# A four-layer graph network: node tables written inside the edge passes, normalizations in halves

## The reference, cut to what matters

```
h = relu(layernorm(x));  x = x + GAT(h)        # two graph attention passes over the edges:
    xl, xr = h @ Wl.T + bl, h @ Wr.T + br
    score  = leaky(xl[src] + xr[dst] + edge_attr @ We.T) @ att
    alpha  = softmax of score over the edges of a target
    out    = segment_sum(alpha * xl[src], dst) + bo
    g = instance_norm(relu(out1));  g = instance_norm(relu(out2(g) + h @ Wskip.T + bskip))
h = relu(layernorm(x));  x = x + GIN(h)        # neighbour sums, MLP, batch norm over the nodes, relu, + h
h = relu(layernorm(x));  x = x + ATT(h)        # attention over the edges, then a layer norm
h = relu(layernorm(x));  x = x + GCN(GCN(h))   # two normalized neighbour sums with an MLP between
```

## Time and profile before

| | us |
|---|---|
| time before, median of 3 runs (lowest to highest) | 6561.05 (6558.09 to 6562.64) |
| profiled execution, its own time | 6555.38 |
| its span from first to last instruction | 6553.5 |
| PE / DVE / ACT / POOL busy | 5634.2 / 4266.8 / 2346.2 / 3061.3 |
| granted TensorE clock, mean share of full speed | 0.947 |

### The profile page before, as it was taken

The page is one execution under the profiler, slowest core; times in us unless marked ns, Lnnn a source line. Parts: engine busy times, 40 slices in busy tenths (PEclk is TensorE's granted clock), DMA queues, the critical chain, the costliest instruction groups (busy, mean ns, idle before and its releaser), DMA issues. The chain is left out here.

```text
span 6553.5 us, 176947 instructions
## 1 busy us (share of the span) xinstructions
PE 5634.2 (86%) x42237; PEld 3858.0 (59%) x42238; DVE 4266.8 (65%) x13369; ACT 2346.2 (36%) x4950; POOL 3061.3 (47%) x3216
## 2 busy tenths in 40 slices
PE   0399999999999938999999999996785999994978
PEld 0366666666666626666666666664773333334978
DVE  5477777777777766777777777776326666665131
ACT  0144444444444414444444444442002444441000
POOL 0177777777777707777777777772000000000000
PEclk9999999999999959999999999997876999996979
DMA  1244444444444414444444444441741222222948
GB/s 47 55 113 106 107 107 109 107 108 107 107 107 108 110 29 109 107 109 107 107 108 108 108 107 107 109 106 36 309 172 40 90 95 90 84 81 104 379 183 308
DMA packets 706049, 768.34 MB, mean 117 GB/s; under 512 B 375941, under 2 KB 628909, under 8 KB 680885
## 3 DMA queue, kind: packets, MB, share of 16 engines
q1 hardware_dynamic: 584087, 583.69, 29.5%
q0 software_dynamic: 102400, 105.06, 8.5%
q10 hardware_dynamic: 19488, 78.68, 3.1%
HBM read 678.14 MB, written 88.81 MB: 117 GB/s over the span
## 5 line engine op out<-in xcount | busy, mean ns | idle before, releaser
L681 POOL DMA_INDIRECT gat_rows<-rows_scr,gat_idx x3200 | 3055.7, 955 | 1334.7 <-issue 1128.9
L727 DVE TENSOR_SCALAR adj_hot_key<-adj_iota_key,adj_winbase,adj_key 128x392 bf16<-128x392 int16 x2416 | 954.0, 395 | 0.0
L927 PE MATMUL gat_sps<-gat_relu,gat_att 128*128 128x256 f32 x3200 | 906.7, 406 | 0.0
L887 PE MATMUL gat_counts<-adj_hot_key,adj_hot_lo 128*128 128x392 bf16 x2416 | 748.0, 335 | 180.2 <-DVE adj_hot_key L727 66.9
L825 ACT ACTIVATE gat_weightsT<-gat_tps 128x512 f32<-128x512 f32 x800 | 477.7, 597 | 1173.0 <-PE gat_tps L937 1162.0
L811 ACT ACTIVATE gat_weights<-gat_masked,gat_newtop 128x512 f32<-128x512 f32 x800 | 577.5, 722 | 877.0 <-DVE gat_newtop L780 745.7
L726 DVE TENSOR_SCALAR adj_hot_lo<-adj_iota_lo,adj_low 128x128 bf16<-128x128 int16 x2416 | 677.4, 280 | 242.4 <-issue 223.3
L944 PE MATMUL gat_aps<-gat_rows,gat_weightsT 128*128 128x65 f32 x6400 | 803.5, 269 | 0.0
L944 PEld LDWEIGHTS gat_aps<-gat_rows,gat_weightsT 128*128 128x128 f32 x6400 | 777.8, 192 | 0.0
L887 PEld LDWEIGHTS gat_counts<-adj_hot_key,adj_hot_lo 128*128 128x128 bf16 x2416 | 232.5, 96 | 751.8 <-DVE adj_hot_key L727 556.3
L912 PE MATMUL gat_mps<-gat_ea,gat_we 128*128 128x256 f32 x1600 | 524.6, 410 | 159.8 <-DMA gat_rows<-rows_scr,gat_idx 147.0
(11 more groups left out here) (320 smaller groups left out, 6969.5 us busy)
## 6 DMA issues: line engine op xcount, KB each, us to landing
gcn_sum_adj<-adj_scr SPq DMA_DIRECT2D x98, 1568.0 KB, 8.5
gat_dstb<-dst_scr SPq DMA_DIRECT2D x800, 128.0 KB
gat_ea<-in_ea SPq DMA_DIRECT2D x800, 128.0 KB
gin_sum_adj<-adj_scr SPq DMA_DIRECT2D x49, 1568.0 KB, 8.3
adj_scr<-adj_tiles ACTq DMA_DIRECT2D x48, 1568.0 KB
at_adj<-adj_scr SPq DMA_DIRECT2D x84, 896.0 KB, 4.8
gat_rows<-rows_scr,gat_idx POOLq DMA_INDIRECT x3200
gat_xr<-xr_scr SPq DMA_DIRECT2D x1600, 24.0 KB
```

Source lines behind the costliest of these rows:

```text
L681: pool.indirect_dma_start(rows[:, u, c, 0:ROW], None, rows_d, bass.IndirectOffsetOnAxis(ap=idx[:, u, c:c + 1], axis=0)).then_inc(s_g[u], 16)
L727: dve.tensor_scalar(plan.hot_key[:, slot, :], plan.iota_key[:], plan.winbase[:, bass.ds(w, 1)], plan.key[:, bass.ds(c, 1)], ALU.add, ALU.i ...
L887: return pe.matmul(bank[:, 0:WD * NT], plan.hot_lo[:, slot, :], plan.hot_key[:, slot, :], start=start, stop=False)
L927: last = pe.matmul(sps[j][:, h * (GE // 2):(h + 1) * (GE // 2)], att[:, h, :], relu[:, j, :], start=True, stop=True)
```

## The change

1. `gat_tables` is gone. `xlr` now lies in the memory of the pass's accumulator `acc`, and `gat_edges` makes the tables itself: SP stores the xl columns straight from `xlr`; DVE splits the xr columns into the memory of the adjacency tiles (`plan.tiles`), with `g` as the scratch array; SP stores the parts from there.
2. The setup is reordered. DVE fills `gat_rows` first and lets POOL go; then it splits; then it fills what is left (six of the fills are dropped, three made smaller). `acc` is cleared after the xl rows have landed.
3. The five loads are parted: `idx` and `dstb` count on `s_id[u]`, for which POOL waits; `ea` and `xr` stay on `s_ld[u]`, for which PE waits. SP issues the group parts of the first eight visits, then waits for the split and stores the xr table, waits until it has landed, then issues the range parts of those eight visits; from the second turn on it issues all five together as before. ScalarE waits for the xr stores, since it writes `plan.tiles`.
4. Layer norm: sums, subtraction and squares in two parts of 25 and 24 tiles; relu_in and the squares on ScalarE; relu_out in one operation with the multiplication.
5. Batch norm: the first square goes; subtraction and squares in two parts, squares on ScalarE; x + h is made on POOL at the start and the last two operations become one.

```diff
+PARTS = [(0, NT // 2 + 1), (NT // 2 + 1, NT)]
 def layer_norm(...):
-            if relu_in:
-                dve.tensor_scalar(src[:], src[:], 0.0, None, ALU.max)
-                dve.drain()
-            dve.tensor_reduce(mean[:, 0:NT], src[:], AX.X, ALU.add)
+            for j, (a, z) in enumerate(PARTS):
+                if relu_in:
+                    dve.wait_ge(s_in, j + 1)
+                dve.tensor_reduce(mean[:, a:z], src[:, a:z, :], AX.X, ALU.add)
...
-            dve.tensor_tensor(dst[:], src[:], per_node(mean), ALU.subtract)
-            dve.drain()
-            dve.tensor_tensor(tmp[:], dst[:], dst[:], ALU.mult)
-            dve.drain()
-            dve.tensor_reduce(var[:, 0:NT], tmp[:], AX.X, ALU.add)
+            for a, z in PARTS:
+                dve.tensor_tensor(dst[:, a:z, :], src[:, a:z, :], of_node(mean, a, z), ALU.subtract).then_inc(s_off, 1)
+            for j, (a, z) in enumerate(PARTS):
+                dve.wait_ge(s_sq, j + 1)
+                dve.tensor_reduce(var[:, a:z], tmp[:, a:z, :], AX.X, ALU.add)
...
-            dve.tensor_tensor(dst[:], dst[:], per_node(rs), ALU.mult)
-            dve.drain()
             if relu_out:
-                dve.tensor_scalar(dst[:], dst[:], 0.0, None, ALU.max)
-                dve.drain()
+                dve.scalar_tensor_tensor(dst[:], dst[:], 0.0, per_node(rs), ALU.max, ALU.mult)
+            else:
+                dve.tensor_tensor(dst[:], dst[:], per_node(rs), ALU.mult)
+            dve.drain()
...
         def _(act):
+            if relu_in:
+                for a, z in PARTS:
+                    act.activation(src[:, a:z, :], src[:, a:z, :], ACT.Relu).then_inc(s_in, 1)
+            for j, (a, z) in enumerate(PARTS):
+                act.wait_ge(s_off, j + 1)
+                act.activation(tmp[:, a:z, :], dst[:, a:z, :], ACT.Square).then_inc(s_sq, 1)
             act.wait_ge(s_var, 1)
             act.activation(sd[:, 0:NT], var[:, 0:NT], ACT.Sqrt).then_inc(s_sd, 1)

-def gat_tables(nc, k, tag, xlr, rows_d, xr_d):
...
 def gat_edges(..., second, xlr, rest):
+        xr3 = plan.tiles[:].rearrange("p s h w d -> p (s h w d)")[:, 0:NT * XR].rearrange("p (t f) -> p t f", f=XR)
...
             sp.wait_ge(s_tab, 16)
-            sp.wait_ge(s_set, 3)
+            sp.dma_start(rows_d.rearrange("(t p) f -> p t f", p=P), xlr[:, :, 0:D]).then_inc(s_rows_out, 16)
...
+            for u in range(RING):
+                load_pair(0, u)
+                group_parts(u)
+            sp.wait_ge(s_xr, 1)
+            sp.dma_start(xr_d[HB:HB + 1, :, :]..., empty_row[:]).then_inc(s_xr_out, 16)
+            for j in range(2):
+                sp.dma_start(xr_d[0:HB, :, :]...[j], xr3[HALF * j:HALF * (j + 1), :, :]).then_inc(s_xr_out, 16)
+            sp.wait_ge(s_xr_out, 48)
+            for u in range(RING):
+                load_pair(0, u)
+                range_parts(u)          # two halves of xr -> s_ld[u]
+            with sp.Fori(1, turns) as i:
                 for u in range(RING):
+                    load_pair(i, u)
+                    sp.wait_ge(s["message"], count("message", i * RING + u, RING))
+                    group_parts(u)
+                    range_parts(u)
...
         def _(pool):
-            pool.wait_ge(s_set, 3)
+            pool.wait_ge(s_ones, 1)
+            pool.wait_ge(s_rows_out, 16)
             with pool.Fori(0, turns) as i:
                 for u in range(RING):
-                    pool.wait_ge(s_ld[u], i * (16 * LOADS) + 16 * LOADS)
+                    pool.wait_ge(s_id[u], i * 32 + 32)
...
         def _(dve):
+            dve.memset(rows[:], 1.0)
             dve.memset(codes[:, VTAB:], IDLE)
+            dve.drain().then_inc(s_ones, 1)
+            dve.sem_inc(s["sum"], FREE)
+            dve.sem_inc(s["message"], FREE)
+            dve.memset(empty_row[:], 0.0)
+            split3(dve, xlr[:, :, D:2 * D], lambda j: xr3[:, :, j * D:(j + 1) * D], rest[:])
+            dve.drain().then_inc(s_xr, 1)
...
+            dve.wait_ge(s_rows_out, 16)
+            dve.memset(acc[:], 0.0)
...
         def _(act):
             act.wait_ge(s_set, 3)
+            act.wait_ge(s_xr_out, 48)
...
         def _(pe):
                     pe.wait_ge(s["relu"], count("relu", step, 2))
+                    pe.nop(nofuse=True)
+                    pe.wait_ge(s_ld[v], i * 48 + 48)
                     pe.wait_ge(s_g[v], i * (16 * GC) + 16 * GC)
                     pe.nop(nofuse=True)

 def batch_norm(...):
-            dve.tensor_tensor(sq[:], z[:], z[:], ALU.mult)
...
-            dve.tensor_tensor(z[:], z[:], wide(bc[:, 0, :]), ALU.subtract)
-            dve.drain()
-            dve.tensor_tensor(sq[:], z[:], z[:], ALU.mult)
-            dve.drain()
+            for a, b in PARTS:
+                dve.tensor_tensor(z[:, a:b, :], ...).then_inc(s_off, 1)
+            dve.wait_ge(s_squared, 2)
...
-            dve.scalar_tensor_tensor(z[:], z[:], 0.0, h[:], ALU.max, ALU.add)
-            dve.drain()
-            dve.tensor_tensor(x[:], x[:], z[:], ALU.add)
+            dve.wait_ge(s_both, 1)
+            dve.scalar_tensor_tensor(x[:], z[:], 0.0, both[:], ALU.max, ALU.add)
...
+        def _(pool):
+            pool.tensor_tensor(both[:], x[:], h[:], ALU.add).then_inc(s_both, 1)
```

More of the change, by code:

```diff
@@ L135, in _, with of_node @@
             pool.memset(iota_node[:, IDLE:HB], float(2 * NP))
+PARTS = [(0, NT // 2 + 1), (NT // 2 + 1, NT)]
 @phase
 def layer_norm(nc, k, tag, src, dst, tmp, st, relu_in=False, relu_out=False, add_to=None):
[L141 removed]
+    s_in, s_off, s_sq, s_var, s_sd = (k.sem(tag + x) for x in ("_in", "_off", "_sq", "_var", "_sd"))
     mean, var, sd, rs = (st[:, j, :] for j in range(4))
+    def of_node(stat, a, z):
+        return stat[:, a:z].unsqueeze(2).to_broadcast([P, z - a, D])
     with nc.Block() as block:
@@ L536, in gat_tables @@
 @phase
[L537 to L567 removed]
 def gat_edges(nc, k, tag, ea_d, src_d, dst16_d, code_d, rows_d, xr_d, we_d, att_d, acc, top, ident,
[L569 removed]
+              iota_node, turns_sb, plan, adj_d, second, xlr, rest):
     names = ("masked", "message", "fifth", "relu", "score", "top", "weight", "turned", "evac", "sum", "acc",
@@ L591, in gat_edges @@
     w_first = second * (NW // 2)
+    s_id = [k.sem(f"{tag}_id{j}") for j in range(RING)]
+    s_ones, s_xr, s_rows_out, s_xr_out = (k.sem(tag + x) for x in ("_ones", "_xr_made", "_rows_out", "_xr_out"))
     s_set, s_tab, s_w = k.sem(tag + "_set"), k.sem(tag + "_tab"), k.sem(tag + "_wts")
@@ new lines, in range_parts @@
+            def range_parts(u):
+                sp.reg_alu(half[1], pair, 16 * (u % 2), ALU.logical_shift_right)
+                sp.reg_alu(half[1], half[1], CODE - 1, ALU.bitwise_and)
+                sp.reg_add(half[0], half[1], 1)
+                sp.reg_alu(half[0], half[0], CODE - 2, ALU.bitwise_and)
+                sp.reg_alu(half[1], half[1], CODE - 2, ALU.bitwise_and)
+                sp.reg_add(half[1], half[1], 1)
+                blocks = [sp.snap(half[0], min_val=0, max_val=HB), sp.snap(half[1], min_val=1, max_val=HB - 1)]
+                for j in range(2):
+                    sp.dma_start(xr[HALF * j:HALF * (j + 1), u, :],
+                                 xr_d[bass.ds(blocks[j], 1), :, :]).then_inc(s_ld[u], 16)
@@ L872, in _ @@
             pe.wait_ge(s_w, 32)
-            for n in ("message", "score", "turned", "sum"):
+            for n in ("score", "turned"):
                 pe.sem_inc(s[n], FREE)
@@ L1204, in batch_norm @@
                                                  ("gb", "sq", "sums", "var", "sd", "row", "bcast"))
+    s_off, s_squared, s_both = (k.sem("bn_" + n) for n in ("off", "squared", "both"))
     lastp = N - (NT - 1) * P
@@ L1208, in batch_norm @@
         sq = sb("sq", [P, NT, D])
+        both = sb("both", [P, NT, D])
         sums = sb("sums", [P, 2, D])
@@ L1270, in _ @@
             pe.matmul(bp[:, 0:2 * D], ones[0:1, :], row[:].rearrange("o a f -> o (a f)"), start=True, stop=True).then_inc(s_bp, 1)
+        @block.gpsimd
+        def _(pool):
+            pool.tensor_tensor(both[:], x[:], h[:], ALU.add).then_inc(s_both, 1)
         @block.scalar
         def _(act):
+            for j, (a, b) in enumerate(PARTS):
+                act.wait_ge(s_off, j + 1)
+                act.activation(sq[:, a:b, :], z[:, a:b, :], ACT.Square).then_inc(s_squared, 1)
             act.wait_ge(s_var, 1)
```

95 lines of the change are left out of this document (27 added, 68 removed).

## The result

The changed kernel takes **6456.78 us** (median of 4 runs, 6429.31 to 6461.31) against 6559.57 (6548.07 to 6562.64) for the kernel before on the same chip: a ratio of 0.9838, with a 95% interval of 0.9808 to 0.9868. The forecast was 6481 with a range of 6464 to 6508.

What follows compares the result with a forecast made beforehand. The DVE-PE hand-over was taken to set the edge passes' pace, with single-engine stages between on the path. Gains 45.4 + 23.8 + 7.3 - 2.4 + 8.8 - 2.6 = 80.3 us; 6561 - 80.3 = 6481, range 6464 to 6508.

Steps and rivals of the forecast that it cites:

- Start of an edge pass: Projection's last copy to first message: PE starts 22.7 us earlier a pass, SP's queue last; 45.4 us for two.
- Inside the visits: Edge-pass loop: PE's added no-op and wait cost 0, covered by DVE's half of the loop.
- gathers that run further ahead buy nothing inside: Edge-pass visits: DVE and PE set the pace of 5.06 us, so earlier gathers on POOL gain nothing there.
- a pace off by over 0.03 us: Sign against the forecast: a visit's pace differing from 5.06 us by more than 0.03 us, 24 us in all.
- Normalizations: Seven layer norms: split squares gain 3.4 us each, 23.8; relu_out's merging 7.3; relu_in's move to ScalarE -2.4.
- the -2.4: Two norms with relu_in on ScalarE: a 1.28 us table load exposed ahead of relu, -2.4 us together.
- Batch normalization: Unused square 3.44 us, split second square 1.8, last addition 3.5: together 8.8 us gained.
- 0, since a reduction of 5.28 comes first: Batch norm: POOL's x + h addition taken to cost nothing; 3.4 us if it held DVE.
- Semaphores: Phase ends: 48 more semaphores at 0.055 us each cost 2.6 us.
- gathers set the pace after all: Rival: POOL's gathers pace the visits, so each pass shrinks by 52 us, not 22.7; 6422 us; chance 0.05.
- PE's extra wait: Rival: wait ahead of messages costs p a visit, 800 p; 6601 us at 0.15; chances 0.03 no change, 0.03 slower.
- SP's one queue eats the gain: Rival: loads blocked behind the rows store or slow xr stores leave 8 us a pass; 6510 us; chance 0.12.

Runs made afterwards that it cites:

- xr_store_on_act: The changed kernel with the three xr table stores issued by ScalarE instead of SP: 7842.64 us under a changing clock, ratio 0.9803 to the kernel before.
- pe_wait_twice: The changed kernel with PE's added no-op and wait ahead of the messages doubled: 7846.13 us under a changing clock, ratio 0.9796 to the kernel before.
- ea_wait_on_pool: The changed kernel with the ea and xr wait back on POOL, PE's added no-op and wait gone: 7879.69 us under a changing clock, ratio 0.9842.
- gathers_late_bn_dve: The changed kernel, POOL waiting once ahead of its loop for the first ea and xr, x + h made on DVE: 7960.64 us, changing clock, ratio 0.9866.
- three_gathers_before: The kernel before with three gathers a visit instead of four: 6588.86 us against 6559.47, ratio 1.0048.
- xr_store_after_four: The changed kernel with SP issuing four visits' group parts ahead of the xr stores, the other four behind: 7849.32 us, changing clock, ratio 0.9817.
- whole_third: The changed kernel run again unaltered, under a changing clock: 7845.7 us against 8000.06 for the kernel before, ratio 0.9806.
- whole_again: The changed kernel run again unaltered, beside its two halves: 6454.25 us against 6559.47 for the kernel before, ratio 0.9842.

## The prediction against this, by its own steps

- *Start of an edge pass, 45.4 us:* right in mechanism, low by 5.9. It is 51.3 us (147.0 - 95.7), and SP's queue was last, as xr_store_on_act shows. The block behind the rows store was as forecast (208.64 to 211.29 + 4.48 = 215.8, 7.1 us). The mis-sized terms are the eight groups, 1.95 us each (from the second idx load at 217.84 to the eighth at 229.52 in six steps) instead of 2.15, and the stretch from the stores' issue to the first message, 20.4 us (231.56 to 251.94) instead of 21.8 (248.9 to 270.7).
- *Inside the visits, 0:* no price of the added wait could be seen, to within 0.03 us a visit and at the changing clock alone (pe_wait_twice, ea_wait_on_pool). **The step that failed is "gathers that run further ahead buy nothing inside", or rather the assumption behind it that the visit's length of 5.06 us is fixed by the work of DVE and PE.** It is not: the visits of the new edge passes took 3 to 4 us less in the first pass and 9 to 15 in the second, with shorter idle times of DVE between the same instructions, and taking work from POOL made them longer by 27 us. That POOL doesn't set the pace was right; that what POOL does has no part in it was wrong. Whether it is the gathers' head start that shortened the visits, as the quoted words would have it, is not shown. The prediction named a pace off by over 0.03 us as a sign against it (it is 0.009 in one pass, 0.037 in the other), but left the range no room for a faster one: its bounds were those of the starts and norms.
- *Normalizations, 23.8 + 7.3 - 2.4:* 3.52 a norm was forecast as 3.4, a ScalarE half takes 1.51 us (L185) where 1.67 was extrapolated. No table load stands between relu and the squares or ahead of relu in the two norms that have it: the -2.4 was wrong, and what "ScalarE: Activation LUTs" of the Trainium skill says in "Table sets: the hidden batching unit" was right; the root's load, as that at 79.91, lies under the reduction.
- *Batch normalization, 8.8:* 7.6 (40.3 to 32.7). The missing 1.2 is mostly the small addition, 1.29 us instead of 0.23, held up until POOL's ends; gathers_late_bn_dve shows the cause. By the rule of the Trainium skill ("SBUF — State Buffer", "Who interferes with whom") an estimated 1.4 us had been worked out, with an addition of 6.9 us; it took 6.96. The measured 1.06 agrees in mechanism. "0, since a reduction of 5.28 comes first" overlooked that POOL is slower than the reduction.
- *Semaphores, 2.6:* between the first norm and the next phase DVE is idle for 0.99 us where it was 0.79, with three semaphores more: 0.07 each instead of 0.055, under 1 us in all if it holds everywhere.
- *Sum:* 5.9 from the starts and 12 to 18 from the visits make 18 to 24 of the 22.5 us missed; norms and batch norm together (37.6 for 36.2) add the little that may be left. Of the rivals, "gathers set the pace after all" is refuted by three_gathers_before and "PE's extra wait" by pe_wait_twice. "SP's one queue eats the gain" did not come true: the block behind the rows store was 7.1 us as before, and the stores took no longer beside the gathers than forecast.

## What to carry to other kernels

A loop of two engines that hand over to each other need not have a fixed length: here it moved by up to 0.04 us in 5.06 with the same instructions, and the 12 to 18 us that this makes are more than most of the terms added up here. A range has to leave room for it, on both sides. When loads are re-ordered at a start, count what is queued behind a store of many small pieces: small loads put behind it wait for it, and moving the store to another engine's queue brought the first message forward without starving anyone. And before two profiles are subtracted, compare one stage that the change doesn't touch: here two projections held 22 us of clock.

## What the runs showed of the hardware

- One gather on POOL took 7.54 us instead of 0.94, from 227.09 to 234.6, while DVE's fill of `acc` ran from 228.31 to 233.7; in xr_store_after_four one took 6.49 us (from 240.52) beside the same fill (240.69, 5.37 us). So it is in both passes of every profile with early gathers (6.47 to 7.55 us). The split's last cast (220.15, 3.42 us), which also runs beside gathers, held none up, nor did the short fills from 223.81 on (0.06 to 0.91 us each). It cost nothing that PE's waits show: the first message was 17 us away (251.94). "SBUF — State Buffer" of the Trainium skill, section "SBUF: two separate sides", describes such a hold: while a DVE instruction in one of its two-port modes runs, POOL can't write the descriptors of a DMA that it issues. The page names a copy there; that one long fill went with such a hold, and the short ones didn't, is what the rows add.
- The same kernel took 6560 us in one group of runs and 8000 in others, with the granted clock changing between its levels through both edge passes (0.91 in the stretch of whole_third shown). A mean clock lower by a tenth went with a quarter fewer matmuls in the same time, 1082 for 1424.
- Removing a quarter of the gathers made the kernel 0.5% slower.
- The same projection ran at the lower level in some executions and mostly at the higher one in others: 143 matmuls in 30.71 us at 0.50 and in 20.31 us at a mean of 0.80. Of the 60 projections in the 20 profiles (two ahead of the passes and the attention's) 55 took 32.2 to 32.6 us from first to last matmul and five 19.7 to 21.9. All five are in the three profiles of the changed kernel itself (two in after, one in whole_again, two in whole_third), none in its variants, though most of these are the same up to the first projection. Why isn't known. The two lowest times of the kernel before, 6548.07 and 6548.33, lie 11 us under its median, the worth of one projection; that this is their cause is a guess.
